# The front of a two-layer transformer kernel, put in another order on every engine

## The chip, the cores and the metric

One Trainium2 chip; the kernel uses one of its cores. The metric is the device time of one execution in microseconds (us), lower is better. All data are float32.

## What is computed

Layer 0 takes x of shape 4 x 1024 x 128 (four chunks of 1024 rows), normalises each row to xn and adds two branches to x: causal attention with 16 heads of 64, and a gated feed-forward block with integer weights.

```python
xn = _layernorm(x)                              # (x - mean) / sqrt(var + eps)
qkv = einsum('bse,ehd->bshd', xn, qkv_w) + qkv_b
attn = softmax(where(mask, q @ k / 8, -large)) @ v
x = x + attn @ out_w + out_b \
      + (silu(xn @ wg.T) * (xn @ wu.T)) @ wd.T  # wg, wu, wd = int / 127, 384 hidden columns
```

Layer 1 (a linear attention with a delta rule, and eight experts of which two are used) follows it. The change does not touch it.

## The kernel before

Every engine has its own list of instructions, written out by hand; semaphores join them. The change lies in the *front* of layer 0: what comes ahead of unit 0 of the attention. The attention has 32 units (4 chunks x 8 pairs of heads), each a call of `unit(u)` on every engine.

The front does the following for each chunk b = 0 to 3; a hidden block is (b, j) with j = 0, 1, 2 (three blocks of 128 of the 384 hidden columns).

- SyncE issues all loads in a fixed order: x of chunk 0 in halves, the integer weights, small rows, x of chunks 1 to 3, `outb_bc`, `w_qk` (two loads, `qk_loaded`), `w_v` and `bv_bc` (`v_loaded`), and so on.
- VectorE `statistics(b)`: mean and variance of the eight groups of 128 rows (L763, L767). GpSimd `deviation(b)`: variance plus eps, to the power -0.5 (L342, L344). VectorE `norm(b)`: eight tensor_scalar (L793) write xn. For chunk 0, `first_half`, `first_deviation` and `first_norm` do this in halves already.
- TensorE `flip_xn(b)`: eight transposes (L890), four into PSUM bank `flips[0]`, four into `flips[1]`. ScalarE `keep_hi(b)` copies each half to `hi_T` rounded to float32r (L534), VectorE `keep_lo(b)` writes the remainder `lo_T` (L805), ScalarE `keep_xnT(b)` the full value to `xnT` (L521, L522) for the attention. For chunk 0, `lo_T` comes from GpSimd (L354).
- TensorE `hidden(b, j)`: a gate product into `pair[0]`, then an up product into `pair[1]`. Each is two matmuls of 512 columns with `hi_T` (L914) and two with `lo_T` (L922); hidden(0,0) alone is in plain float32 (L910). ScalarE `silu(b, j)` reads `pair[0]` and writes `act_gate` (L540). VectorE `multiply(b, j)` multiplies `pair[1]` by it (L812). There is one `act_gate` and one pair of banks, so the next gate product waits for the silu, the next silu and the next up product wait for the multiply.
- TensorE `branch(b, halves)`: the down projection of a chunk, 12 small matmuls for each half (L936), into the two `flips` banks (chunk 3: `accum`). VectorE `add_branch` adds each half to x (L819, `ffn_added`). GpSimd `add_bias(b)` adds `out_b` to x first (L348). `flip_xn(b)` for b >= 2 waits for the additions of chunk b - 2, which free the two banks. The branches of chunks 2 and 3 run inside unit 0.
- TensorE `project(0, c, half)` (L959) and `project_values(0, i)` (L972): the six projections of unit 0, all through the one bank `misc`. Their readers are `keep_part` (ScalarE L444 or VectorE L606) and `keep_values` (VectorE L633); each projection waits for the reader of the one ahead of it. unit 0 starts with `project(1, 0, 1)` and then the scores (L994).

Of the kernel before, what the change touches and what calls it, by code (L numbers as in the profile page):

```python
# [6 lines left out]
F32 = mybir.dt.float32  # L7
# [3 lines left out]
ALU = mybir.AluOpType  # L11
ACT = mybir.ActivationFunctionType
# [4 lines left out]
B, S = 4, 1024  # L17
# [135 lines left out]
def layer0(block, sem, sbuf, kept, early, shared, b2_sb, x, qkv_w, qkv_b, out_w, out_b, w_gate, w_up, w_down, ln_w, ln_b, w_slow, w_out, Wg, b1, late):  # L153
# [55 lines left out]
    with ctx:  # L209
# [110 lines left out]
        def _(pool):  # L320
# [19 lines left out]
            def deviation(b):  # L340
                pool.wait_ge(var_ready, b + 1)
                pool.tensor_tensor(rstd[:, b, :], mv[:, b, :, 1], eps[:], ALU.add).then_inc(pool_step, 1)  # L342
                pool.wait_ge(pool_step, b + 2)
                pool.tensor_tensor(rstd[:, b, :], rstd[:, b, :], minus_half[:], ALU.pow).then_inc(rstd_ready, 1)  # L344

            def add_bias(b):
                pool.wait_ge(xn_ready, min(b + 2, B))
                pool.tensor_tensor(x1[:, b, :, :], x1[:, b, :, :],  # L348
                                   outb_bc[:].unsqueeze(1).broadcast_to([P, ROWS, E]), ALU.add).then_inc(xob_ready, 1)
# [3 lines left out]
            pool.wait_ge(hi_kept, 1)  # L353
            pool.tensor_tensor(lo_T[0][:], xnT[:, 0, :], hi_T[0][:].bitcast(F32), ALU.subtract).then_inc(lo_pool, 1)  # L354
            pool.wait_ge(small_loaded, 16)
            for b in range(1, B):
                deviation(b)
                add_bias(b - 1)
            add_bias(B - 1)

# [55 lines left out]
        def _(act):  # L416
# [100 lines left out]
            def keep_xnT(b):  # L517
                act.wait_ge(xn_flipped, 2 * b + 2)
                if b:
                    act.wait_ge(lo_dve, 2 * b)  # L520
                    act.activation(xnT[:, b, 0:512], flips[0][:], ACT.Copy)  # L521
                act.activation(xnT[:, b, 512:1024], flips[1][:], ACT.Copy).then_inc(xnT_act, 1)  # L522

            def keep_hi(b):
                if b == 0:
                    act.wait_ge(xnT_dve, 1)
                    act.wait_ge(xnT_act, 1)
                    act.activation(hi_T[0][:], xnT[:, 0, :], ACT.Copy).then_inc(hi_kept, 1)
                    return
                if b >= 2:  # L530
                    act.wait_ge(up_ready, NHID * (b - 1))
                for f in range(2):
                    act.wait_ge(xn_flipped, 2 * b + f + 1)
                    act.activation(hi_T[b % 2][:, 512 * f:512 * (f + 1)], flips[f][:], ACT.Copy).then_inc(hi_kept, 1)  # L534

            def silu(b, j):
# [3 lines left out]
                act.activation(act_gate[:], pair[0][:], ACT.Silu, scale=INT_SCALE).then_inc(silu_ready, 1)  # L540

            act.wait_ge(ints_loaded, 48)
            act.activation(raw_f[:, 0:2, :], raw[:, 0:2, :], ACT.Copy)
# [17 lines left out]
            keep_xnT(2)  # L561
            act.wait_ge(bq_scaled, 1)
            silu(2, 0)
            silu(2, 1)
            keep_hi(3)
            silu(2, 2)
            keep_xnT(3)
            silu(3, 0)
            keep_part(0, 1, 1)
            silu(3, 1)  # L570
            keep_part(0, 0, 0)
            silu(3, 2)
            for u in range(UNITS):
# [4 lines left out]
        def _(dve):  # L578
# [208 lines left out]

            def norm(b):
                dve.wait_ge(rstd_ready, b + 1)
                if b >= 2:  # L790
                    dve.wait_ge(xn_flipped, 2 * (b - 1))
                for r in range(ROWS):
                    last = dve.tensor_scalar(xn[:, b % 2, r, :], x1[:, b, r, :], mv[:, b, r, 0:1], rstd[:, b, r:r + 1],  # L793
                                             ALU.subtract, ALU.mult)
                last.then_inc(xn_ready, 1)
# [4 lines left out]

            def keep_lo(b):
                for f in range(2):
                    part = slice(512 * f, 512 * (f + 1))
                    dve.wait_ge(hi_kept, 2 * b + f)
                    dve.tensor_tensor(lo_T[b % 2][:, part], flips[f][:], hi_T[b % 2][:, part].bitcast(F32), ALU.subtract).then_inc(lo_dve, 1)  # L805

# [23 lines left out]
            dve.tensor_scalar(bq8, bq8, SCALE, None, ALU.mult).then_inc(bq_scaled, 1)  # L830
            statistics(1)
            multiply(0, 0)
            norm(1)
            multiply(0, 1)
            keep_lo(1)
            statistics(2)
            multiply(0, 2)
            norm(2)
            multiply(1, 0)
            add_branch(0, (0,))  # L840
            multiply(1, 1)
            add_branch(0, (1,))
            keep_lo(2)
            dve.wait_ge(v_loaded, 32)
            dve.wait_ge(bq_scaled, 1)
            statistics(3)
            multiply(1, 2)
            norm(3)
            multiply(2, 0)
            keep_part(0, 0, 1)  # L850
            add_branch(1, (0,))
            multiply(2, 1)
            add_branch(1, (1,))
            keep_part(0, 1, 0)
            keep_lo(3)
            multiply(2, 2)
            keep_values(0, 0)
# [9 lines left out]
        def _(pe):  # L867
# [12 lines left out]

            def flip_xn(b):
                if b:
                    pe.wait_ge(xn_ready, b + 1)
                if b >= 2:
                    pe.wait_ge(ffn_added, 2 * (b - 1))
                for f in range(2):
                    if b == 0:
                        pe.wait_ge((xn_first, xn_ready)[f], 1)
                    for r in range(GB):
                        last = pe.transpose(flips[f][:, P * r:P * (r + 1)], xn[:, b % 2, GB * f + r, :], ident[:])  # L890
                    last.then_inc(xn_flipped, 1)

            def hidden(b, j):
                n = b * NHID + j
                for h, w_T in enumerate((gate_T, up_T)):
                    if h == 0 and n:
# [235 lines left out]
            hidden(0, 0)  # L1132
            hidden(0, 1)
            flip_xn(1)
            hidden(0, 2)
            hidden(1, 0)
            pe.wait_ge(xnT_act, 2)
            branch(0, (0,))
            hidden(1, 1)
            branch(0, (1,))  # L1140
            flip_xn(2)
            hidden(1, 2)
            pe.wait_ge(qk_loaded, 32)
            pe.wait_ge(v_loaded, 32)
            project(0, 0, 1)
            hidden(2, 0)
            pe.wait_ge(xnT_act, 3)
            branch(1, (0,))
            hidden(2, 1)
            branch(1, (1,))  # L1150
            project(0, 1, 0)
            flip_xn(3)
            hidden(2, 2)
            project_values(0, 0)
            pe.wait_ge(xnT_act, 4)
            hidden(3, 0)
            project_values(0, 1)
            project(0, 1, 1)
            hidden(3, 1)
            project(0, 0, 0)  # L1160
            hidden(3, 2)
            pe.wait_ge(outw_loaded, 16)
# [2089 lines left out]
```

## Time and profile before

| what | value |
|---|---|
| time, median of 3 runs | 1658.24 us (1657.25 to 1658.27) |
| time of the profiled execution | 1658.69 us |
| its span | 1657.0 us |
| TensorE busy over the span | 1636.4 us (99%) |
| VectorE, ScalarE, GpSimd busy | 1328.9, 1006.7, 888.1 us |
| first transpose of xn | 9.44 us |
| first score of unit 0 | 66.78 us |

The profile is one execution on the chip. Busy time of TensorE counts each matmul to its modelled end, so two matmuls in a row overlap a little; a timeline row gives the start of a group, the time until the end of its last instruction, the engine, the line, what it writes and reads, the number of instructions (a float32 matmul is counted once for each of its passes), and in brackets how long the engine was idle before it and what ended that.

### The profile page before, as it was taken

How to read it: one execution, taken by the hardware profiler on the slowest of the kernel's cores; microseconds unless marked ns; L12 is line 12 of the kernel's file. 1: busy time of each engine (PE TensorE's matmuls, PEld its weight loads, DVE VectorE, ACT ScalarE, POOL GpSimd, SP SyncE). 2: the span in 40 equal slices, each digit the busy share in tenths (PEclk: the TensorE clock that was granted, in tenths of full speed). 3: DMA queues.
4: the chain of work that ended last, by engine and by line, in shares of the span. 5: the costliest groups of instructions: out<-in, count | busy, mean ns of one | idle time of the engine just before them, and what ended most of it. 6: DMA issues, size and time to landing. Idle time of an engine off the chain costs nothing.

```text
span 1657.0 us, 29205 instructions
## 1 busy us (share of the span) xinstructions
PE 1636.4 (99%) x9922; PEld 1043.9 (63%) x9922; DVE 1328.9 (80%) x2763; ACT 1006.7 (61%) x2025; POOL 888.1 (54%) x686
## 2 busy tenths in 40 slices
PE   8999999999999999999999999999999999999998
PEld 6756556655665566566656665665666767676767
DVE  6677777777777778777777777776999999999997
ACT  4456666656665666566656666666676657566562
POOL 3233333334333333433333433334999999999995
PEclk9999999999999999999999999999999999999999
DMA  8000000000000000000000000000000000000000
GB/s 182 26 1 1 2 1 1 1 2 1 1 1 1 1 2 1 1 1 1 1 1 1 1 2 1 1 27 1 1 1 7 7 1 8 5 4 7 1 8 13
DMA packets 30036, 13.55 MB, mean 8 GB/s; under 512 B 17066, under 2 KB 29380, under 8 KB 29892
## 3 DMA queue, kind: packets, MB, share of 16 engines
q1 hardware_dynamic: 29892, 11.70, 3.0%
q8 instruction: 82, 1.34, 0.3%
q14 instruction: 62, 0.51, 0.1%
HBM read 9.60 MB, written 2.10 MB: 7 GB/s over the span
## 4 chain that ended last, share of the span: by engine, by line
PE 92%; DVE 4%; ACT 1%; issue 1%; POOL 1%; DMA 0%; SPq 0%; DVEq 0%; ACTq 0%; POOLq 0%
PE pair L994 17%; PE flip L1011 16%; PE accum L1032 11%; PE pair L2739 8%; PE misc L959 7%; PE flip L2762 4%; PE misc L1078 4%; PE flip L2751 4%; PE misc L972 3%; PE accum L1056 3%; PE flip L2799 3%; PE accum L2751 2%; PE accum L2762 2%; PE accum L1060 2%; PE flip L2785 1%; PE flip L936 1%
## 5 line engine op out<-in xcount | busy, mean ns | idle before, releaser
L388 POOL TENSOR_SCALAR probs<-probs,recip 128x256 f32<-128x256 f32 (+5 forms) x448 | 331.3, 754 | 687.5 <-DVE recip L642 687.4
L463 ACT ACTIVATE probs<-pair,neg_max 128x768 f32<-128x768 f32 (+5 forms) x448 | 332.0, 749 | 208.4 <-DVE neg_max L624 208.4
L624 DVE TENSOR_REDUCE neg_max<-pair 128x1 f32<-128x768 f32 (+7 forms) x512 | 372.8, 754 | 31.4 <-PE pair L994 9.5
L1011 PEld LDWEIGHTS flip<-ident,probs 128*128 128x128 f32 x2048 | 228.0, 141 | 142.3 <-issue 64.7
L994 PE MATMUL pair<-qk_sb 64*128 64x512 f32 (+3 forms) x1536 | 291.6, 505 | 1.4 <-ACT probs L463 0.7
L1011 PE MATMUL flip<-ident,probs 128*128 128x128 f32 x2048 | 280.0, 277 | 1.8 <-ACT slots L425 1.8
L425 ACT ACTIVATE slots<-flip 128x512 f32<-128x512 f32 x320 | 183.6, 595 | 155.5 <-PE flip L1011 155.5
L615 DVE TENSOR_TENSOR pair<-pair,mask 128x128 f32<-128x128 f32 x512 | 137.2, 292 | 80.4 <-PE pair L994 80.3
L1032 PE MATMUL accum<-slots,v_sb 128*64 128x512 f32 (+3 forms) x1024 | 192.7, 519 | 0.0
L2739 PE MATMUL pair<-slow_sb,h_T 128*128 128x512 f32 x384 | 180.0, 594 | 1.2 <-ACT probs_last L463 1.0
L1571 POOL TENSOR_TENSOR prod<-xnT,qs 128x1024 f32<-128x1024 f32 (+3 forms) x32 | 180.2, 5638 | 0.9 <-DVE qs L2280 0.9
L994 PEld LDWEIGHTS pair<-qk_sb 64*128 64x128 f32 x1536 | 123.0, 186 | 69.3 <-issue 44.6
L1032 PEld LDWEIGHTS accum<-slots,v_sb 128*64 128x64 f32 x1024 | 67.9, 136 | 136.9 <-issue 132.3
L587 DVE COPY slots<-flip 128x512 f32<-128x512 f32 x192 | 131.9, 687 | 21.2 <-PE flip L1011 18.3
L959 PE MATMUL misc<-xnT,w_qk 128*128 128x512 f32 x256 | 134.3, 606 | 1.2 <-DVE v_sb L633 1.2
L2739 PEld LDWEIGHTS pair<-slow_sb,h_T 128*128 128x128 f32 x384 | 69.4, 190 | 74.1 <-issue 66.3
L1563 POOL TENSOR_TENSOR prod<-xnT 128x1024 f32<-128x1024 f32 (+2 forms) x24 | 109.2, 4551 | 10.5 <-DVE xnT L2280 10.2
L1609 POOL TENSOR_TENSOR terms<-terms 128x1024 f32<-128x1024 f32 x42 | 99.3, 2365 | 3.2 <-DVE terms L2366 1.2
L2762 PEld LDWEIGHTS flip<-w_qk,hid 128*128 128x128 f32 x736 | 87.3, 192 | 13.7 <-issue 8.4
L2762 PE MATMUL flip<-w_qk,hid 128*128 128x128 f32 x736 | 90.5, 276 | 0.2
L463 ACT ACTIVATION_READ_ACCUMULATOR probs<-pair,neg_max 128x1 f32 x448 | 90.5, 202 | 0.0
L2320 DVE TENSOR_REDUCE misc<-prod 128x16 f32<-128x1024 f32 (+3 forms) x32 | 90.2, 2818 | 0.0
(230 smaller groups left out, 2539.7 us busy)
## 6 DMA issues: line engine op xcount, KB each, us to landing
out<-x SPq DMA_DIRECT2D x8, 256.0 KB, 2.3
x<-in_L_attn_x SPq DMA_DIRECT2D x3, 512.0 KB, 5.8
slow_sb<-in_L_attn_w_slow SPq DMA_DIRECT2D x3, 512.0 KB, 7.5
w_qk<-in_L_attn_qkv_w SPq DMA_DIRECT2D x2, 512.0 KB, 7.2
xn<-in_L_ffn_W SPq DMA_DIRECT2D x1, 1024.0 KB
x<-in_L_attn_x SPq DMA_DIRECT2D x2, 256.0 KB, 3.3
w_v<-in_L_attn_qkv_w SPq DMA_DIRECT2D x1, 512.0 KB, 7.5
bv_bc<-in_L_attn_qkv_b SPq DMA_DIRECT2D x1, 512.0 KB, 7.5
```

The costliest lines, as they stand in the source:

```text
L388: pool.tensor_scalar(part, part, recip[:, u % 2, row, h:h + 1], 0.0, ALU.mult, ALU.add).then_inc(scaled, 1)
L425: act.activation(slot_rows(step, h, f), flips[bank][:].rearrange("p (k q) -> p k q", q=P), ACT.Copy).then_inc(flip_kept[bank], 1)
L463: act.activation(dst, pair[h][:, lo:hi], ACT.Exp, bias=neg_max[:, u % 2, row, h:h + 1], accum_out=row_sum[:, u % 2, row, h:h + 1]).then_in ...
L615: dve.tensor_tensor(pair[h][:, hi - P:hi], pair[h][:, hi - P:hi], mask[:], ALU.add).then_inc(covered, 1)
L624: dve.tensor_reduce(out=neg_max[:, u % 2, row, h:h + 1], in_=pair[h][:, lo:hi], axis=AX.X, op=ALU.max, negate=True).then_inc(max_ready, 1)
L959: pe.matmul(misc[:], lhsT=w_qk[:, c, P * n:P * (n + 1)], rhs=xnT[:, u // PAIRS, 512 * half:512 * (half + 1)], start=True, stop=True).then_ ...
L994: last = pe.matmul(pair[h][:, a:z], lhsT=q[part, P * r:P * (r + 1)], rhs=k[part, a - lo:z - lo], start=True, stop=True)
L1011: last = pe.transpose(flips[bank][:, P * k:P * (k + 1)], src[:, P * k:P * (k + 1)], ident[:])
L1032: last = pe.matmul(accum[D * h:D * (h + 1), at:512], lhsT=values_of(u, k, h), rhs=slots[:, base + at:base + 512], start=k == 0, stop=k == ...
L1571: pool.tensor_tensor(prod[s % 2][:, s:2 * s + 1, :], ks[:, 0:s + 1, :], qs[:, s % 2:s % 2 + 1, :].broadcast_to([P, s + 1, HD]), ALU.mult). ...
L2739: last = pe.matmul(places[k][:, 512 * half:512 * (half + 1)], lhsT=h_T[:, P * s:P * (s + 1)], rhs=slow_sb[:, c, 512 * half:512 * (half + 1 ...
L2762: last = pe.matmul(places[k][:, P * s:P * (s + 1)], lhsT=hid[:, e % 2, j, P * s:P * (s + 1)], rhs=w2_sb[:, e, j, :], start=j == 0, stop=j ...
```

## The change

The arithmetic is the same. The lists of the front are put in another order on every engine:

- VectorE: `norm` and `keep_lo` take one half at a time (the steps stand next to each other still; each half has its own semaphore count). `statistics(2)` moves from behind `keep_lo(1)` to a place ahead of `multiply(0,0)`, `statistics(3)` from behind `keep_lo(2)` to one behind `multiply(0,2)`. `keep_part(0,0,1)` and `keep_part(0,1,0)` move forward.
- TensorE: `flip_xn(b)` waits for each half of `norm` and for each half's bank alone. A `hidden` block can be issued as gate and up product apart: the transposes of chunk 1 stand between gate and up of (0,2); the second halves of the branches of chunks 0 and 1 stand between gate and up of (1,1) and (2,1), ahead of the up product; the transposes of chunks 2 and 3 come behind that up product. The projections of unit 0 are at other places, the last one, `project(0,0,0)`, at the very end.
- ScalarE: a Silu of one column of `ident` stands first. `keep_part(0,1,1)` and `keep_part(0,0,0)` come each one silu later.
- GpSimd: `deviation(1)` and `deviation(2)` come ahead of the biases; the biases wait for their own chunk's norm only.

```diff
--- before.py
+++ after.py
@@ -344,7 +344,7 @@
                 pool.tensor_tensor(rstd[:, b, :], rstd[:, b, :], minus_half[:], ALU.pow).then_inc(rstd_ready, 1)
 
             def add_bias(b):
-                pool.wait_ge(xn_ready, min(b + 2, B))
+                pool.wait_ge(xn_ready, 2 * b + 1)
                 pool.tensor_tensor(x1[:, b, :, :], x1[:, b, :, :],
                                    outb_bc[:].unsqueeze(1).broadcast_to([P, ROWS, E]), ALU.add).then_inc(xob_ready, 1)
 
@@ -352,11 +352,14 @@
             first_deviation(1)
             pool.wait_ge(hi_kept, 1)
             pool.tensor_tensor(lo_T[0][:], xnT[:, 0, :], hi_T[0][:].bitcast(F32), ALU.subtract).then_inc(lo_pool, 1)
+            deviation(1)
+            deviation(2)
             pool.wait_ge(small_loaded, 16)
-            for b in range(1, B):
-                deviation(b)
-                add_bias(b - 1)
-            add_bias(B - 1)
+            add_bias(0)
+            add_bias(1)
+            deviation(3)
+            add_bias(2)
+            add_bias(3)
 
             def constants():
                 pool.memset(earlier[:], 1.0).then_inc(earlier_step, 1)
@@ -521,7 +524,7 @@
                     act.activation(xnT[:, b, 0:512], flips[0][:], ACT.Copy)
                 act.activation(xnT[:, b, 512:1024], flips[1][:], ACT.Copy).then_inc(xnT_act, 1)
 
-            def keep_hi(b):
+            def keep_hi(b, halves=(0, 1)):
                 if b == 0:
                     act.wait_ge(xnT_dve, 1)
                     act.wait_ge(xnT_act, 1)
@@ -529,7 +532,7 @@
                     return
                 if b >= 2:
                     act.wait_ge(up_ready, NHID * (b - 1))
-                for f in range(2):
+                for f in halves:
                     act.wait_ge(xn_flipped, 2 * b + f + 1)
                     act.activation(hi_T[b % 2][:, 512 * f:512 * (f + 1)], flips[f][:], ACT.Copy).then_inc(hi_kept, 1)
 
@@ -539,6 +542,8 @@
                     act.wait_ge(hid_kept, b * NHID + j)
                 act.activation(act_gate[:], pair[0][:], ACT.Silu, scale=INT_SCALE).then_inc(silu_ready, 1)
 
+            act.wait_ge(ident_made, 1)
+            act.activation(act_gate[:, 0:1], ident[:, 0:1], ACT.Silu)
             act.wait_ge(ints_loaded, 48)
             act.activation(raw_f[:, 0:2, :], raw[:, 0:2, :], ACT.Copy)
             act.activation(raw_f[:, 2, :], raw[:, 2, :], ACT.Copy, scale=INT_SCALE * INT_SCALE).then_inc(ints_scaled, 1)
@@ -559,17 +564,17 @@
             keep_hi(2)
             silu(1, 2)
             keep_xnT(2)
-            act.wait_ge(bq_scaled, 1)
             silu(2, 0)
             silu(2, 1)
             keep_hi(3)
             silu(2, 2)
             keep_xnT(3)
+            act.wait_ge(bq_scaled, 1)
             silu(3, 0)
+            silu(3, 1)
             keep_part(0, 1, 1)
-            silu(3, 1)
+            silu(3, 2)
             keep_part(0, 0, 0)
-            silu(3, 2)
             for u in range(UNITS):
                 unit(u)
             tails["scalar"] = keep_flip, keep_att
@@ -785,11 +790,11 @@
                                              ALU.subtract, ALU.mult)
                 last.then_inc((xn_first, xn_ready)[f], 1)
 
-            def norm(b):
+            def norm(b, f):
                 dve.wait_ge(rstd_ready, b + 1)
                 if b >= 2:
                     dve.wait_ge(xn_flipped, 2 * (b - 1))
-                for r in range(ROWS):
+                for r in range(GB * f, GB * (f + 1)):
                     last = dve.tensor_scalar(xn[:, b % 2, r, :], x1[:, b, r, :], mv[:, b, r, 0:1], rstd[:, b, r:r + 1],
                                              ALU.subtract, ALU.mult)
                 last.then_inc(xn_ready, 1)
@@ -798,11 +803,10 @@
                 dve.wait_ge(xn_flipped, 2 * b + 1)
                 dve.tensor_copy(xnT[:, b, 0:512], flips[0][:]).then_inc(xnT_dve, 1)
 
-            def keep_lo(b):
-                for f in range(2):
-                    part = slice(512 * f, 512 * (f + 1))
-                    dve.wait_ge(hi_kept, 2 * b + f)
-                    dve.tensor_tensor(lo_T[b % 2][:, part], flips[f][:], hi_T[b % 2][:, part].bitcast(F32), ALU.subtract).then_inc(lo_dve, 1)
+            def keep_lo(b, f):
+                part = slice(512 * f, 512 * (f + 1))
+                dve.wait_ge(hi_kept, 2 * b + f)
+                dve.tensor_tensor(lo_T[b % 2][:, part], flips[f][:], hi_T[b % 2][:, part].bitcast(F32), ALU.subtract).then_inc(lo_dve, 1)
 
             def multiply(b, j):
                 dve.wait_ge(silu_ready, b * NHID + j + 1)
@@ -829,31 +833,37 @@
             dve.wait_ge(columns_kept, 1)
             dve.tensor_scalar(bq8, bq8, SCALE, None, ALU.mult).then_inc(bq_scaled, 1)
             statistics(1)
+            statistics(2)
             multiply(0, 0)
-            norm(1)
+            norm(1, 0)
+            norm(1, 1)
             multiply(0, 1)
-            keep_lo(1)
-            statistics(2)
+            keep_lo(1, 0)
+            keep_lo(1, 1)
             multiply(0, 2)
-            norm(2)
+            statistics(3)
+            norm(2, 0)
+            norm(2, 1)
             multiply(1, 0)
             add_branch(0, (0,))
+            dve.wait_ge(bq_scaled, 1)
+            keep_part(0, 0, 1)
+            add_branch(0, (1,))
             multiply(1, 1)
-            add_branch(0, (1,))
-            keep_lo(2)
+            keep_lo(2, 0)
+            keep_lo(2, 1)
+            multiply(1, 2)
+            norm(3, 0)
+            norm(3, 1)
+            multiply(2, 0)
+            add_branch(1, (0,))
+            keep_part(0, 1, 0)
+            add_branch(1, (1,))
+            multiply(2, 1)
+            keep_lo(3, 0)
+            keep_lo(3, 1)
+            multiply(2, 2)
             dve.wait_ge(v_loaded, 32)
-            dve.wait_ge(bq_scaled, 1)
-            statistics(3)
-            multiply(1, 2)
-            norm(3)
-            multiply(2, 0)
-            keep_part(0, 0, 1)
-            add_branch(1, (0,))
-            multiply(2, 1)
-            add_branch(1, (1,))
-            keep_part(0, 1, 0)
-            keep_lo(3)
-            multiply(2, 2)
             keep_values(0, 0)
             multiply(3, 0)
             keep_values(0, 1)
@@ -878,21 +888,24 @@
                 pe.transpose(pair[1][:, j * P:(j + 1) * P], raw_f[:, 2, j * P:(j + 1) * P], ident[:])
             pe.transpose(pair[1][:, 512:512 + COLUMNS], stage[:], ident[0:COLUMNS, 0:COLUMNS]).then_inc(setup_flipped, 1)
 
-            def flip_xn(b):
-                if b:
-                    pe.wait_ge(xn_ready, b + 1)
-                if b >= 2:
-                    pe.wait_ge(ffn_added, 2 * (b - 1))
-                for f in range(2):
+            def flip_xn(b, halves=(0, 1)):
+                for f in halves:
                     if b == 0:
                         pe.wait_ge((xn_first, xn_ready)[f], 1)
+                    else:
+                        pe.wait_ge(xn_ready, 2 * b + f)
+                    if b == 1:
+                        pe.wait_ge((xnT_dve, xnT_act)[f], 1)
+                    elif b:
+                        pe.wait_ge(ffn_added, 2 * (b - 2) + f + 1)
                     for r in range(GB):
                         last = pe.transpose(flips[f][:, P * r:P * (r + 1)], xn[:, b % 2, GB * f + r, :], ident[:])
                     last.then_inc(xn_flipped, 1)
 
-            def hidden(b, j):
+            def hidden(b, j, products=(0, 1)):
                 n = b * NHID + j
-                for h, w_T in enumerate((gate_T, up_T)):
+                for h in products:
+                    w_T = (gate_T, up_T)[h]
                     if h == 0 and n:
                         pe.wait_ge(silu_ready, n)
                     elif h and n:
@@ -1131,34 +1144,37 @@
             flip_xn(0)
             hidden(0, 0)
             hidden(0, 1)
+            hidden(0, 2, (0,))
             flip_xn(1)
-            hidden(0, 2)
+            hidden(0, 2, (1,))
+            pe.wait_ge(qk_loaded, 32)
+            project(0, 0, 1)
             hidden(1, 0)
             pe.wait_ge(xnT_act, 2)
             branch(0, (0,))
-            hidden(1, 1)
+            hidden(1, 1, (0,))
             branch(0, (1,))
+            hidden(1, 1, (1,))
             flip_xn(2)
             hidden(1, 2)
-            pe.wait_ge(qk_loaded, 32)
-            pe.wait_ge(v_loaded, 32)
-            project(0, 0, 1)
+            project(0, 1, 0)
             hidden(2, 0)
             pe.wait_ge(xnT_act, 3)
             branch(1, (0,))
-            hidden(2, 1)
+            hidden(2, 1, (0,))
             branch(1, (1,))
-            project(0, 1, 0)
+            hidden(2, 1, (1,))
             flip_xn(3)
             hidden(2, 2)
+            pe.wait_ge(v_loaded, 32)
             project_values(0, 0)
-            pe.wait_ge(xnT_act, 4)
             hidden(3, 0)
             project_values(0, 1)
+            hidden(3, 1)
             project(0, 1, 1)
-            hidden(3, 1)
+            hidden(3, 2)
             project(0, 0, 0)
-            hidden(3, 2)
+            pe.wait_ge(xnT_act, 4)
             pe.wait_ge(outw_loaded, 16)
             for u in range(UNITS):
                 unit(u)
```

## Rows read from the trace of the kernel before

**Rows 1.** Windows: us, busy by engine (x instructions), clock, DMA share, GB/s.

```profile
25.00:29.00 4.00, 3.97 (x17) 3.58 (x18) 3.08 (x9) 1.02 (x1) 1.74 (x2) 0.58 1.21 222
9.44:66.78 57.34, 48.62 (x243) 36.17 (x243) 37.41 (x102) 24.84 (x33) 18.73 (x15) 0.97 0.59 121
100.00:200.00 100.00, 100.00 (x643) 60.38 (x643) 74.39 (x163) 62.03 (x144) 35.07 (x48) 1.00 0.01 1
```

**Rows 2.** Timeline of TensorE in the front: start, us, then as told above.

```profile
14.88 0.73 PE L914 MATMUL pair<-hi_T,gate_T 128*128 128x512 f32 x2 [0.24 <-ACT act_gate L540]
...
19.03 1.09 PE L890 MATMUL flip<-ident,xn 128*128 128x128 f32 x8 [1.69 <-DVE xn L793]
19.88 0.71 PE L914 MATMUL pair<-hi_T,gate_T 128*128 128x512 f32 x2
...
25.03 1.22 PE L914 MATMUL pair<-hi_T,up_T 128*128 128x512 f32 x2 [1.67 <-DVE slots L812]
...
32.15 2.84 PE L936 MATMUL flip<-down_T,slots 128*128 128x128 f32 x24
35.93 1.06 PE L890 MATMUL flip<-ident,xn 128*128 128x128 f32 x8 [0.95 <-DVE x L819]
...
41.97 0.73 PE L914 MATMUL pair<-hi_T,up_T 128*128 128x512 f32 x2 [1.31 <-DVE slots L812]
...
47.55 2.84 PE L936 MATMUL flip<-down_T,slots 128*128 128x128 f32 x24
50.22 1.02 PE L959 MATMUL misc<-xnT,w_qk 128*128 128x512 f32 x2
...
62.41 1.02 PE L959 MATMUL misc<-xnT,w_qk 128*128 128x512 f32 x2
...
65.14 1.02 PE L959 MATMUL misc<-xnT,w_qk 128*128 128x512 f32 x2
66.78 1.99 PE L994 MATMUL pair<-qk_sb 64*128 64x512 f32 x8 [0.63 <-issue]
```

**Rows 3.** Timeline of ScalarE in the front.

```profile
12.51 1.28 ACT L540 ACT_TABLE_LOAD   x1
13.80 1.02 ACT L540 ACTIVATE act_gate<-pair 128x1024 f32<-128x1024 f32 x1
...
21.09 1.03 ACT L540 ACTIVATE act_gate<-pair 128x1024 f32<-128x1024 f32 x1 [0.28 <-PE pair L922]
...
63.48 0.69 ACT L444 ACTIVATE qk_sb<-misc,columns 128x512 f32<-128x512 f32 x1 [0.77 <-PE misc L959]
```

**Rows 4.** Timeline of VectorE in the front.

```profile
14.86 1.23 DVE L812 TENSOR_TENSOR slots<-pair,act_gate 128x1024 f32<-128x1024 f32 x1 [1.49 <-ACT act_gate L540]
16.83 2.14 DVE L793 TENSOR_SCALAR xn<-x,mv,rstd 128x128 f32<-128x128 f32 x8 [0.74 <-POOL rstd L344]
...
20.35 1.29 DVE L805 TENSOR_TENSOR lo_T<-flip,hi_T 128x512 fp32r<-128x512 f32 x2 [0.25 <-ACT hi_T L534]
21.56 1.64 DVE L763 BATCH_NORM_STATS2 stats<-x 128x6 f32<-128x128 f32 x8
...
23.79 1.19 DVE L812 TENSOR_TENSOR slots<-pair,act_gate 128x1024 f32<-128x1024 f32 x1
```

**Rows 5.** Timeline of GpSimd in the front.

```profile
15.16 1.64 POOL L344 TENSOR_TENSOR rstd<-rstd,minus_half 128x8 f32<-128x8 f32 x1
```

**Rows 6.** Loads of chunks 1 to 3, and of w_qk (second half).

```profile
L302 SPq DMA_DIRECT2D x<-in_L_attn_x x3: 393/574/1587, 6.2 to 7.2; - x3
...
DMA to landing us min/median/max: 4.4/5.8/6.9
...
11.21 2.95 SPq L305 DMA_DIRECT2D w_qk<-in_L_attn_qkv_w  x1
...
w_qk<-in_L_attn_qkv_w SPq DMA_DIRECT2D x1, 512.0 KB, 8.1
```

**Rows 7.** Line 784 from 6.6 to 7.84 us (ns min/median/max).

```profile
L784 DVE TENSOR_SCALAR xn<-x,mv,rstd x4: 343/348/350, 6.6 to 7.4; 128x128 f32<-128x128 f32 x4
```

## The prediction

> **What bounds the kernel now.** I read busy time and granted clock by stretches first, then TensorE's timeline, then the other engines' over the same stretch. From 100 to 200 us TensorE is busy for all of the 100 us [rows 1]: there the kernel ends when TensorE has worked through its list, so what is saved ahead of that list is saved at the end. The front, from the first transpose of xn at 9.44 us to the first score of unit 0 at 66.78, is different: TensorE is busy for 48.62 of 57.34 us, and from 25 to 29 us its mean clock was 0.58 of full speed, which costs 4.0 x 0.42 = 1.7 us [rows 1]. Its timeline shows the stops in brackets: 1.69 us for the xn of chunk 1, 1.67 us for a multiply of VectorE, 0.95 for a branch addition, 1.31 for another multiply [rows 2]. All changed lines are in this front, and behind it every engine has the list that it had. So the question is when the first score of unit 0 starts, against 66.78.
>
> **Prices of TensorE's work**, from start to start in full flow. A projection and a whole hidden block are 65.14 - 62.41 = 2.73 us, half a branch 50.22 - 47.55 = 2.67, the transposes of a chunk 19.88 - 19.03 = 0.85 [rows 2]. A projection ends 1.02 after its start, 0.16 of that as the tail that the next one overlaps (a two-pass row starts again 0.43 later twice): 0.86. So a hidden block is 1.87, one of its two products (gate or up, high and low part) 0.94; a value projection moves as many columns as a projection, 0.86. After a stop, the flow runs about 0.1 behind these: up(2,0), two half branches and a block are 8.15 by them and took 50.22 - 41.97 = 8.25.
>
> **Prices of the hand-overs.** Gate start to silu start 21.09 - 19.88 = 1.21, and the same from up start to a multiply that waits for it; silu to multiply 14.86 - 13.80 = 1.06; silu to the next gate 14.88 - 13.80 = 1.08; multiply to the up product behind it 25.03 - 23.79 = 1.24 [rows 2 to 4]. VectorE: statistics 23.79 - 21.56 = 2.23, norm 2.14 less 0.09 overlap = 2.05, a half 1.03; both lo_T halves 21.56 - 20.35 = 1.21; a multiply 1.23, less the same overlap 1.14 [rows 4].
>
> **ScalarE's table.** The one-column Silu loads Silu's table while ScalarE waits for the integers, and the load of 1.28 us at 12.51 goes [rows 3]. silu(0,0) then starts with the gate product instead of at 13.80. On the path it gives at most the 0.24 us that TensorE waited at 14.88 [rows 2], and the next stop takes that back.
>
> **Statistics moved.** statistics(1) ends at 14.86 - 1.49 = 13.37 [rows 4]. statistics(2) now follows it, until 15.53, ahead of multiply(0,0), which slips from 14.86. A loss of 0.67 for up(0,1): 15.53 + 1.24 = 16.77; silu(0,1) 16.85, gate(0,2) 17.93. The norm of chunk 1 does not slip: it had waited 0.74 us for rstd until 16.83 [rows 4], and VectorE is free at 16.67. So norm(1) stands at 16.83, multiply(0,1) at 18.88 as before; there the loss ends. This holds if x of chunk 2 has landed by 13.3: the loads of chunks 1 to 3 are issued between 6.2 and 7.2 and land 4.4, 5.8 and 6.9 us later, the middle one about 12.4 [rows 6]. Spare 0.9.
>
> **First turn of TensorE.** gate(0,2), now ahead of the transposes, runs 17.93 to 18.87, the transposes to 19.72 (their first half is ready at 17.9, the second at 18.9), up(0,2) waits for multiply(0,1): 18.88 + 1.24 = 20.12. The transposes come 0.16 earlier than before, so hi_T is done at 21.09 - 0.28 - 0.16 = 20.65, where silu(0,2) starts, and lo_T at 21.40 [rows 3, 4]. multiply(0,2) no longer stands behind statistics(2): 20.65 + 1.06 = 21.7 instead of 23.79. TensorE meanwhile does up(0,2) to 21.06, the projection moved here to 21.92 (the second half of w_qk is issued at 11.21 and takes 8.1, there by 19.3 [rows 6]) and gate(1,0) to 22.86. up(1,0) starts at 21.7 + 1.24 = 22.9 and was at 25.03: 2.1 us, with a projection of 0.86 already done. Lead 3.0.
>
> **From 23.84 on** I walked every wait of the new lists. TensorE's work up to the last projection of unit 0 is four half branches 10.68, four single products 3.76, six hidden blocks 11.22, five projections 4.30, two sets of transposes 1.70, together 31.66: to 55.5 if nothing waits. The narrow places:
> First, multiply(1,0) stands behind statistics(3) and norm(2): 22.84 + 2.23 + 2.05 = 27.1, so up(1,1) could start at 28.4. TensorE has both half branches and a gate in between and comes at 30.1. Spare 1.8.
> Second, the second half of the transposes of a chunk needs the addition behind the half branch: 35.93 - 32.15 = 3.78 after that branch starts [rows 2]. Between the two lie now the branch, an up product and half the transposes, 2.67 + 0.94 + 0.43 = 4.04. Spare 0.26, for chunks 2 and 3; before, TensorE stood for 3.78 - 2.67 = 1.1.
> Third, from a gate to the next up by way of silu and multiply it is 1.21 + 1.06 + 1.24 = 3.51. Between them lie gate, up, a projection or values, gate: 3 x 0.94 + 0.86 = 3.68. Spare 0.17, at up(2,0), (3,0), (3,1) and (3,2). At up(1,2) and (2,2) it is up to up, 1.21 + 1.24 = 2.45, against 0.94 + 0.85 + 0.94: spare 0.28. In the old list statistics(3) sat in such a gap, and TensorE stood for 1.31 at 41.97 [rows 2].
> Fourth, the tail. The last projection of unit 0 starts at 54.7; ScalarE begins to empty its bank 63.48 - 62.41 = 1.07 later and takes 0.69 [rows 2, 3]. The first projection of unit 1 needs that bank, with no hidden block in between as before: a new wait of 0.95, until 56.5. It is over at 57.4; multiply(3,2), which held the score back at 66.78, is done by 56.4.
>
> **Sum.** The score starts at 57.4, with 0.1 for each of three restarts at 57.7: 66.78 - 57.7 = 9.1 us. A cross-check by losses: before, 8.7 idle, 0.16 more of tail at each of ten stops, 1.7 for the clock, 12.0; after, 0.6 at the start, 1.35 before up(0,1), 0.2, 0.4, 0.04 and 0.95, 3.5: a gain of 8.5. I take the walk. The profiled execution lasted 1658.69 us, 1.7 around its span of 1657.0; less 9.1 that is 1649.6. It ran 0.45 above the median of the runs: 1649.1.
> Bounds: with no stop at all TensorE's 44.2 us of work from 9.5 would give 53.7, so 13 us is the most. Downwards, six narrow places that each miss by 0.2 cost 1.2.
>
> **Rivals.**
> The clock. It fell right after two stops of 1.69 and 1.67 us in 8 us [rows 1, 2]. The new order has one of 1.35, then gaps under 0.5, then 0.95 alone; the old one had 1.31 alone, at full clock behind it. So I expect no fall; one that stays costs the same 1.7 and gives 1650.8. The Trainium skill (TensorE: Matmul & The Clock Gate, section "HAM oscillation") says that bursts of matmuls with waits between them can run throttled again and again; by that rule this front stays at risk, for the same price, and this trace agrees with it once.
> The path that VectorE and GpSimd share. The power of deviation(2), 1.64 us [rows 5], now runs beside norm(1), which is on the path. If it held VectorE for its length, all behind slips: 1650.7. Against it: four norms that ran from 6.6 us, beside the power of chunk 0's second half, took 343 to 350 ns each [rows 7], eight with GpSimd idle 2.14 together, no less. The Trainium skill (SBUF — State Buffer, section "SBUF: two separate sides") calls this path an exclusive lock between a two-port VectorE operation and GpSimd; that is this rival, and the trace does not bear it out for the power.
> Slower. statistics(2) puts a load ahead of multiply(0,0) in VectorE's queue, and each us by which chunk 2 lands after 13.3 moves the whole front by one. Landing in 8.1 us like w_qk it would cost 1.4; it decides only past 26.0 (9.1 + 3.3 more). Nothing in [rows 6] comes near.
> Nothing gained. The lead would have to go again, 6 us of it: 14 us at 0.58 of the clock. Or unit 0 gives it back; but its waits are on engines that all come earlier by the same amount.
>
> **How the numbers follow.** Forecast (score between 56.7 and 58.7) 0.60, its own range 1648.1 to 1650.1; the clock 0.12; narrow places late or a wait that I missed, 1 to 4 us, 0.13; shared path 0.03; nothing gained 0.06; slower 0.03; more gained, through shorter early stops, 0.03. A measurement of this kernel tells about 0.2%, 3.3 us, from no change: faster 0.91, same 0.06, slower 0.03. The range takes in the clock, the shared path and most of the narrow places: 1646.9 to 1652.2.
>
> **What would show it.** One table load less and silu(0,0) ahead of 13.8; up(0,1) later, at 16.8; transposes of chunk 1 at 18.9; up(1,0) at 22.9; transposes of chunk 2 near 31.1; the score of unit 0 at 57.7, behind a wait of 0.8 to 0.95 us for ScalarE's qk_sb; granted clock 1.00 throughout. I am wrong if TensorE shows new waits for multiplies between 30 and 55 us, if the clock falls, or if the stretch from that score to the end is longer than the 1590.2 us of before.

## The result, and the profile after

The changed kernel takes 1652.78 us (median of 6 runs, 1651.76 to 1653.82) against 1658.05 us (6 runs, 1657.25 to 1659.37): a ratio of 0.9969, 95% interval 0.9959 to 0.9979. It is faster, by 5.3 us (0.3%), where 9.1 were forecast; the time lies 0.6 us above the range.

TensorE's timeline of the changed kernel, from the first transpose of xn; the lines answer to [rows 2]:

```profile
9.54 1.09 PE L902 MATMUL flip<-ident,xn 128*128 128x128 f32 x8
...
17.05 0.73 PE L927 MATMUL pair<-hi_T,up_T 128*128 128x512 f32 x2 [1.20 <-DVE slots L816]
...
19.21 0.60 PE L902 MATMUL flip<-ident,xn 128*128 128x128 f32 x4
21.30 0.66 PE L902 MATMUL flip<-ident,xn 128*128 128x128 f32 x4 [1.49 <-DVE xn L798]
22.43 0.84 PE L927 MATMUL pair<-hi_T,up_T 128*128 128x512 f32 x2 [0.48 <-DVE slots L816]
...
23.92 1.91 PE L972 MATMUL misc<-xnT,w_qk 128*128 128x512 f32 x2
...
26.88 0.63 PE L927 MATMUL pair<-hi_T,up_T 128*128 128x512 f32 x2
...
35.04 1.03 PE L902 MATMUL flip<-ident,xn 128*128 128x128 f32 x8
...
47.73 1.04 PE L902 MATMUL flip<-ident,xn 128*128 128x128 f32 x8
...
60.55 1.10 PE L972 MATMUL misc<-xnT,w_qk 128*128 128x512 f32 x2 [0.87 <-ACT qk_sb L447]
61.58 1.99 PE L1007 MATMUL pair<-qk_sb 64*128 64x512 f32 x8
```

The score of unit 0 starts at 61.58, not 57.7. Since the loads land earlier or later in each execution, I compare the *front* from here on: first transpose of xn to first score, in the one profiled execution of each kernel. It was 57.34 us, the walk said 57.7 - 9.44 = 48.26, and it is 61.58 - 9.54 = 52.04. All of the 3.8 us too many arise before 26.88, where up(1,0) (the up product of block (1,0)) starts, forecast for 22.9. Behind it the walk holds: from there to the score it said 34.8 us and it took 34.7, with no stop but the one of 0.87 in the tail. The stops that [rows 2] show before the transposes of chunk 2 and before up(2,0) are gone.

What went wrong before 26.88 is in two other timelines. VectorE's:

```profile
13.56 1.65 DVE L768 BATCH_NORM_STATS2 stats<-x 128x6 f32<-128x128 f32 x8
...
15.80 1.19 DVE L816 TENSOR_TENSOR slots<-pair,act_gate 128x1024 f32<-128x1024 f32 x1
16.97 4.28 DVE L798 TENSOR_SCALAR xn<-x,mv,rstd 128x128 f32<-128x128 f32 x8
21.17 1.21 DVE L816 TENSOR_TENSOR slots<-pair,act_gate 128x1024 f32<-128x1024 f32 x1
```

norm(1) takes 4.28 us, and took 2.14 [rows 4]. The same line from 18.6 to 19 us (ns, minimum, median, maximum) shows that it is one instruction:

```profile
L798 DVE TENSOR_SCALAR xn<-x,mv,rstd x2: 340/1406/2473, 18.5 to 18.8; 128x128 f32<-128x128 f32 x2
```

One tensor_scalar of 128 by 128 lasted 2473 ns; the one ahead of it took 340. GpSimd's timeline has what ran beside it:

```profile
17.18 1.72 POOL L344 TENSOR_TENSOR rstd<-rstd,minus_half 128x8 f32<-128x8 f32 x1
18.79 2.38 POOL L348 TENSOR_TENSOR x<-x,outb_bc 128x1024 f32<-128x1024 f32 x1
21.32 2.39 POOL L348 TENSOR_TENSOR x<-x,outb_bc 128x1024 f32<-128x1024 f32 x1 [0.16 <-DVE xn L798]
```

The bias of chunk 0 starts at 18.79 and ends at 21.17; the held instruction ends at 21.25, so it began at 18.78, within 0.01 us of the bias. Without the hold it would have ended at 16.97 + 2.14 = 19.11, that is, 0.3 us into the bias. The power of deviation(2), from 17.18, lay beside seven tensor_scalars of 337 to 347 ns and held none.

The clock fell as well. TensorE alone, in windows of 1 us (length, busy time with the instructions, granted clock, DMA share, GB/s):

```profile
20.00:21.00 1.00, 0.00 (x0) 1.00 1.32 216
22.00:23.00 1.00, 0.57 (x2) 0.95 1.00 196
23.00:24.00 1.00, 1.00 (x4) 0.50 1.04 223
25.00:26.00 1.00, 1.00 (x2) 0.50 1.23 259
26.00:27.00 1.00, 1.00 (x5) 0.84 1.37 230
```

It is at 0.50, the 1.2 GHz level, from just before 23 to about 26.3 us, behind a stretch in which TensorE stood for 1.49 and 0.48 us. Of the six executions three have a mean clock of 0.999 and spans of 1651.0 to 1651.1 us, three 1.000 and 1649.5 to 1649.8: a fall comes in some, and costs about 1.5 us. The profiled one is of the first kind; where the other two have theirs, no trace shows.

### The profile page after: what moved, and what is told of

Read it like the earlier page. It is cut to its first block, busy times and chain, and to the rows that moved or that the text cites. A ratio compares the mean times of both kernels' runs of the same rounds, so it can differ in the third digit from the quotient of the medians.

```text
span 1651.1 us, 29212 instructions
## 1 busy us (share of the span) xinstructions
PE 1635.6 (99%) x9922; PEld 1044.6 (63%) x9922; DVE 1330.1 (81%) x2763; ACT 1005.6 (61%) x2025; POOL 888.1 (54%) x686
## 4 chain that ended last, share of the span: by engine, by line
PE 96%; DVE 2%; ACT 1%; issue 1%; POOL 0%; DVEq 0%; POOLq 0%; ACTq 0%
PE pair L1007 17%; PE flip L1024 17%; PE accum L1045 11%; PE pair L2755 9%; PE misc L972 7%; PE flip L2778 5%; PE misc L1091 4%; PE flip L2767 4%; PE misc L985 3%; PE accum L1069 3%; PE flip L2815 3%; PE accum L2767 2%; PE accum L2778 2%; PE accum L1073 2%; PE flip L2801 1%; PE flip L949 1%
```

## The experiments

Ten kernels ran. Theory A: a tensor_scalar of norm(1) that meets the bias of GpSimd waits until this ends (2.2 us on the path), and the stops behind that let the clock fall (1.6 us). Rival B: the power of deviation(2) does it. The table has the measured values: medians over all runs of a kernel, and the rest from its one profiled execution. The expectations and edits follow. The kernel before ran beside the experiments too, with medians of 1658.2 to 1658.7 us.

| kernel | median us (runs) | front us | norm(1) us | held instruction ns |
|---|---|---|---|---|
| before | 1658.05 (6) | 57.34 | 2.14 | none |
| changed | 1652.78 (6) | 52.04 | 4.28 | 2473 |
| e1_bias_held | 1650.07 (5) | 48.42 | 2.14 | none |
| e2_bias_first | 1652.77 (5) | 51.97 | 4.20 | 2401 |
| e3_old_bias_early | 1660.23 (11) | 58.62 | 4.16 | 2361 |
| e5_filled_stop | 1652.02 (5) | 50.48 | 4.31 | 2502 |
| e9_bias_in_halves | 1650.98 (5) | 49.36 | 3.20 | 1403 |
| e4_held_and_tail | 1649.49 (5) | 48.12 | 2.14 | none |
| e6_no_preload | 1649.97 (5) | 48.44 | 2.14 | none |
| e7_statistics_back | 1651.65 (5) | 50.14 | 2.14 | 1166, in norm(2) |
| e8_branch_whole | 1653.43 (5) | 50.65 | 2.15 | none |
| e10_third_statistics_back | 1651.57 (5) | 50.07 | 2.14 | none |

**e1_bias_held.**

```diff
             def add_bias(b):
-                pool.wait_ge(xn_ready, 2 * b + 1)
+                pool.wait_ge(xn_ready, 3 if b == 0 else 2 * b + 1)
```

> The changed kernel, with one wait moved: GpSimd's bias of chunk 0 waits until both halves of norm(1) are done. Theory A (the bias, 2.38 us long, shut VectorE out of one tensor_scalar of norm(1)): all eight take 0.34 us, norm(1) 2.1 us instead of 4.28, multiply(0,1) at 19.0 instead of 21.17, and the score of unit 0 at 59.4 if the half-clock stretch at 23 to 26 us stays, at 57.8 if it goes: median 1650.6 or about 1649.5. Rival B (the power of deviation(2), which still runs beside norm(1), does it): norm(1) stays at 4.2 us and the time at 1652.8.

VectorE and GpSimd in e1:

```profile
17.51 2.14 DVE L798 TENSOR_SCALAR xn<-x,mv,rstd 128x128 f32<-128x128 f32 x8
19.56 1.22 DVE L816 TENSOR_TENSOR slots<-pair,act_gate 128x1024 f32<-128x1024 f32 x1
```

```profile
17.72 1.72 POOL L344 TENSOR_TENSOR rstd<-rstd,minus_half 128x8 f32<-128x8 f32 x1
19.80 4.74 POOL L348 TENSOR_TENSOR x<-x,outb_bc 128x1024 f32<-128x1024 f32 x2 [0.36 <-DVE xn L798]
```

The power still runs beside norm(1), whose eight take 339 to 346 ns. B falls; the bias is the cause. The front is 48.42 us, 0.2 from the walk, and the mean clock was 1.000 in all five executions. The spans of the two profiled executions differ by 3.0 us only and not by the 3.6 of the fronts, since the first transpose came at 10.09 here and at 9.54 there. Ratio to the kernel before 0.9949 (0.9936 to 0.9961).

**e2_bias_first.** On GpSimd, the bias ahead of deviation(2):

```diff
             deviation(1)
-            deviation(2)
             pool.wait_ge(small_loaded, 16)
             add_bias(0)
+            deviation(2)
             add_bias(1)
```

> The changed kernel with the bias of chunk 0 ahead of deviation(2) on GpSimd, so that the bias and not the power runs beside the start of norm(1). Theory A: one tensor_scalar of norm(1), now an early one, takes 2.4 to 2.7 us, norm(1) again 4.3; time as the changed kernel, within 1 us of 1652.8. Rival B (it is the power): norm(1) 2.1 us, 2 to 4 us faster.

The held instruction is now the first of norm(1):

```profile
L798 DVE TENSOR_SCALAR xn<-x,mv,rstd x1: 2401/2401/2401, 16.8 to 16.8; 128x128 f32<-128x128 f32 x1
```

```profile
16.68 2.39 POOL L348 TENSOR_TENSOR x<-x,outb_bc 128x1024 f32<-128x1024 f32 x1
```

The bias ends at 19.07, and only then do the other seven follow, at 333 to 334 ns. As A said: the hold goes with the bias, wherever it meets the norm.

**e3_old_bias_early.** The kernel before, with that one wait taken from the change:

```diff
-                pool.wait_ge(xn_ready, min(b + 2, B))
+                pool.wait_ge(xn_ready, b + 1 if b == 0 else min(b + 2, B))
```

> The kernel before, with one wait changed: the bias of chunk 0 no longer waits for norm(1) but for norm(0), so it starts at 16.8 beside norm(1). Theory A: a tensor_scalar of norm(1) takes about 2.5 us, norm(1) 4.3 instead of 2.14, the transposes of chunk 1 at 21.2 instead of 19.03, and the kernel is 2 us slower (1660). Rival B: norm(1) 2.1, same time as before.

```profile
17.05 4.16 DVE L793 TENSOR_SCALAR xn<-x,mv,rstd 128x128 f32<-128x128 f32 x8 [0.76 <-POOL rstd L344]
```

```profile
21.26 1.97 PE L890 MATMUL flip<-ident,xn 128*128 128x128 f32 x8 [3.72 <-DVE xn L793]
```

1660.23 us against 1658.34 (16 runs), ratio 1.0010 (1.0001 to 1.0019): 1.9 slower. The profiled front is 1.3 us longer and not 2: the stop before the transposes grew from 1.69 to 3.72, but the one before up(1,0) shrank from 1.67 to 0.33, and the clock was at 0.50 from 20 to 26 us (in before from 25 to 28). By itself this line of the change is a loss, and it is enough for the hold. The old wait for the *next* norm had kept the two apart.

**e5_filled_stop.** The changed kernel; seven matmuls into the unused `accum` between the two halves of the transposes of chunk 1:

```diff
                     last.then_inc(xn_flipped, 1)
+                    if b == 1 and f == 0:
+                        for _ in range(7):
+                            pe.matmul(accum[:, 0:P], lhsT=ident[:], rhs=ident[:], start=True, stop=True)
```

> The changed kernel as it is, bias beside norm(1), with seven matmuls of ident by ident (about 1.5 us, result unused) between the two halves of the transposes of chunk 1, where TensorE stood 1.49 us. Theory A (the held tensor_scalar costs the path 2.2 us by itself, and the stops behind it let the clock fall, 1.6 us more): norm(1) stays 4.2 us, multiply(0,1) at 21.2, but the clock stays at 1.00 from 22 to 27 us, the score comes 1.6 us earlier than 61.58 and every timed execution has the short span, about 1649.5, so a median near 1651.9. Rival: the clock falls all the same, time as the changed kernel (1652.8) or later.

```profile
19.44 1.73 PE L906 MATMUL accum<-ident 128*128 128x128 f32 x14
21.12 0.66 PE L902 MATMUL flip<-ident,xn 128*128 128x128 f32 x4
22.25 0.73 PE L930 MATMUL pair<-hi_T,up_T 128*128 128x512 f32 x2 [0.47 <-DVE slots L816]
22.82 0.63 PE L938 MATMUL pair<-lo_T,up_T 128*128 128x512 f32 x2
23.29 1.02 PE L975 MATMUL misc<-xnT,w_qk 128*128 128x512 f32 x2
```

```profile
23.00:24.00 1.00, 1.00 (x5) 1.00 0.74 167
```

The hold stays (2502 ns), the clock does not fall in this front: it is at 1.00, and the projection's two passes take 1.02 us where they took 1.91. The front is 50.48 us, so that the clock is 52.04 - 50.48 = 1.56 and the hold 50.48 - 48.42 = 2.06 of the 3.6 us between the changed kernel and e1. The spans say the same: 1649.4 to 1650.4 us in the four executions of e5 with the full clock, 1649.5 to 1649.8 in the three of the changed kernel. The median fell by 0.8 us, as expected, since half of the changed kernel's executions had no fall; the runs of the two kernels overlap. I expected the full clock in every execution; the fifth (0.999, span 1651.5) has a fall that no trace places. By itself this run does not show that the filled stop kept the clock up, since half of the executions of the changed kernel have no fall either; more on this below.

**e9_bias_in_halves.** The changed kernel, each bias in two instructions of 128 by 512:

```diff
-                pool.tensor_tensor(x1[:, b, :, :], x1[:, b, :, :],
-                                   outb_bc[:].unsqueeze(1).broadcast_to([P, ROWS, E]), ALU.add).then_inc(xob_ready, 1)
+                for f in range(2):
+                    rows = x1[:, b, GB * f:GB * (f + 1), :]
+                    last = pool.tensor_tensor(rows, rows, outb_bc[:].unsqueeze(1).broadcast_to([P, GB, E]), ALU.add)
+                last.then_inc(xob_ready, 1)
```

> The changed kernel with every bias of GpSimd in two instructions of 128 by 512 instead of one of 128 by 1024; the first still starts beside the last tensor_scalars of norm(1), at 18.8 us. Theory A (a tensor_scalar that starts beside the bias waits until that one instruction of GpSimd ends): the held tensor_scalar takes about 1.2 + 0.1 us instead of 2.47, norm(1) 3.1 instead of 4.28, the front is 1.1 us shorter than the changed kernel's 52.0, and more if the clock stays up. Rival (VectorE is slowed in proportion while GpSimd works, or held for the whole bias): norm(1) 4.2 us as before, since the two halves together last as long.

```profile
L800 DVE TENSOR_SCALAR xn<-x,mv,rstd x2: 341/872/1403, 18.4 to 18.7; 128x128 f32<-128x128 f32 x2
```

```profile
18.68 5.04 POOL L350 TENSOR_TENSOR x<-x,outb_bc 128x512 f32<-128x512 f32 x4
```

One such half starts 5.04 / 4 = 1.26 us behind the one ahead of it and lasts 1.27 to 1.31, and the hold is 1.40: it ends with the one instruction of GpSimd, not with the bias. VectorE is not slowed in proportion, it waits for one instruction. The front is 2.7 us shorter than that of the changed kernel: 1.1 by the shorter hold, and the clock stayed up. This profiled execution has its clock fall outside the front:

```profile
1135.00:1140.00 5.00, 5.00 (x9) 0.67 0.01 3
```

**e4_held_and_tail.** e1, and in the tail:

```diff
-            hidden(3, 2)
+            hidden(3, 2, (0,))
             project(0, 0, 0)
+            hidden(3, 2, (1,))
```

> e1_bias_held, and in the tail the up product of (3,2) behind the last projection instead of ahead of it. The wait of 0.87 us of the first projection of unit 1 for ScalarE's qk_sb goes, but the multiply of (3,2) comes 0.86 later and then holds the score. By the walk the score comes 0.4 to 0.6 us earlier than in e1. Rival: the later multiply eats all of it, no difference to e1.

```profile
56.44 1.10 PE L972 MATMUL misc<-xnT,w_qk 128*128 128x512 f32 x2
57.95 1.99 PE L1007 MATMUL pair<-qk_sb 64*128 64x512 f32 x8 [0.40 <-issue]
```

The stop of 0.87 is gone and TensorE stands for 0.40 before the score. The profile names no releaser for it; the multiply of (3,2) ends at 57.85, 0.1 us ahead of the score. The front is 0.3 shorter, where I expected 0.4 to 0.6, the median 0.6 lower, 1649.49 us, ratio 0.9945 (0.9933 to 0.9958). It has the lowest median; against e1 the difference is less than the runs can tell.

**The other parts, each undone in e1.** e6 leaves out the one-column Silu:

```diff
-            act.wait_ge(ident_made, 1)
-            act.activation(act_gate[:, 0:1], ident[:, 0:1], ACT.Silu)
```

> e1_bias_held without the one-column Silu at the start of ScalarE's list. By the walk the table load comes back at 12.5 us and silu(0,0) at 13.9, before the place where VectorE's statistics(2) let multiply(0,0) run (15.8): no difference to e1_bias_held, within 0.3 us. Rival: the load was on the path, 1 us slower.

The load is back at 13.20, and TensorE stands for 0.24 and 0.87 us where it stood for 1.21 at once; the front is 48.44 against 48.42. Nothing, as expected.

e7 puts statistics(2) back (and, on GpSimd, deviation(2) behind the first bias):

```diff
             statistics(1)
-            statistics(2)
             multiply(0, 0)
...
             keep_lo(1, 1)
+            statistics(2)
             multiply(0, 2)
```

> e1_bias_held with statistics(2) back behind the lo_T of chunk 1 and deviation(2) behind the first bias. By the walk up(0,1) comes 0.7 earlier but multiply(0,2) 2.2 later, about 24 us, so TensorE waits 2 us for it before up(1,0): score 2.1 later than e1 if the clock stays, 3.5 if it falls; median 1652.2 to 1653.7. Rival: the stop is absorbed by work moved there, below 1 us.

```profile
25.04 0.73 PE L927 MATMUL pair<-hi_T,up_T 128*128 128x512 f32 x2 [1.53 <-DVE slots L816]
```

1.7 us of front and 1.6 in the median, where I expected 2.1 or more: the transposes' first half now starts with the first half of norm(1), lo_T is done 0.3 us sooner against the start of the front, and the statistics with it; I had not counted that. By the way it shows the hold once more, off the path: its norm(2) starts at 27.13 beside the second bias, and one tensor_scalar of eight lasts 1166 ns, until that bias is over.

```profile
L798 DVE TENSOR_SCALAR xn<-x,mv,rstd x8: 333/336/1166, 27.1 to 29.8; 128x128 f32<-128x128 f32 x8
```

```profile
25.86 2.35 POOL L348 TENSOR_TENSOR x<-x,outb_bc 128x1024 f32<-128x1024 f32 x1
```

e8 keeps the blocks (1,1) and (2,1) whole:

```diff
-            hidden(1, 1, (0,))
+            hidden(1, 1)
             branch(0, (1,))
-            hidden(1, 1, (1,))
```

(the branch of chunk 1 likewise; on VectorE multiply(1,1) and (2,1) ahead of the second addition)

> e1_bias_held with the gate and up products of (1,1) and (2,1) together again ahead of the second half branch (and VectorE's multiply ahead of the addition). By the walk TensorE then waits 1.1 us before the second half of the transposes needs the addition, less 0.4 because the first half no longer waits, for two chunks: 1.4 to 2.2 us slower than e1. Rival: no difference.

```profile
29.00 0.73 PE L927 MATMUL pair<-hi_T,up_T 128*128 128x512 f32 x2 [0.58 <-DVE slots L816]
...
33.83 0.63 PE L902 MATMUL flip<-ident,xn 128*128 128x128 f32 x4 [0.51 <-DVE x L823]
```

2.2 us of front: half a microsecond and its tail for each pair of transposes, and a stop at up(1,1), since multiply(1,0) behind statistics(3) and norm(2) is no longer covered. I expected 1.4 to 2.2. The median is 3.4 higher; two of the five executions had a clock fall, the profiled one at 1135 to 1140 us as in e9, so the front is the better measure.

e10 puts statistics(3) back behind the lo_T of chunk 2 (and, on GpSimd, deviation(3) behind the bias of chunk 2; only VectorE's part is shown):

> e1_bias_held with statistics(3) back behind the lo_T of chunk 2, ahead of multiply(1,2), and deviation(3) behind the bias of chunk 2. By the walk multiply(1,2) comes 2.2 us later and TensorE, which had 0.14 to spare there, waits some 1.5 to 2.0 us before up(2,0): front 50.0 to 50.4 us instead of 48.4, median 1651.6 to 1652.1. Rival: the gap is covered by the projection that now lies there, under 1 us.

```diff
             multiply(0, 2)
-            statistics(3)
             norm(2, 0)
...
             keep_lo(2, 1)
+            statistics(3)
             multiply(1, 2)
```

```profile
38.10 0.73 PE L927 MATMUL pair<-hi_T,up_T 128*128 128x512 f32 x2 [1.37 <-DVE slots L816]
```

1.65 us of front, 1.5 in the median, as expected.

## Why the prediction was wrong

**The step that failed** is the sentence "So norm(1) stands at 16.83 and multiply(0,1) at 18.88 as before; there the loss ends". The start of norm(1) was right (16.97); its length was not: 4.28 us, where the sum has 2.05, and multiply(0,1) came at 21.17 instead of 18.88. The prediction has no term for the new wait of the bias, and I never wrote down when the bias now starts. The trace of before would have told: deviation(1) ends at 15.16 + 1.64 = 16.80 [rows 5], and deviation(2) took 24.23 + 1.65 - 23.95 = 1.93 there:

```profile
23.95 0.20 POOL L342 TENSOR_TENSOR rstd<-mv,eps 128x8 f32<-128x8 f32 x1 [2.50 <-DVE mv L767]
24.23 1.65 POOL L344 TENSOR_TENSOR rstd<-rstd,minus_half 128x8 f32<-128x8 f32 x1
```

The bias would follow at 18.7, while norm(1) runs until 18.9 by the forecast. They overlap by 0.2 us by these numbers and by 0.3 in the run, and that is enough, because the last tensor_scalar is not slowed for that time but held until the 2.38 us of the bias are over. The rival of the shared path was named, but with the wrong partner: I asked only about the power, which the trace rightly cleared, and gave the rival 0.03. [rows 4] could not warn, since in the old list the bias always waited for the next norm. The rule that I quoted did: the Trainium skill (SBUF — State Buffer, section "SBUF: two separate sides") says that whichever operation starts first keeps the path for its whole instruction, and that the other is blocked. For the bias the runs agree: in the changed kernel, e2, e3, e5 and e9 the held instruction ended about 0.1 us behind the instruction of GpSimd. For the power of 128 by 8 they do not: it ran 1.72 us beside tensor_scalars of normal length.

**The clock** was the second miss, a rival held at 0.12. Its size is 1.56 us by e5, 1.7 by my price. That it follows from the hold is supported, not proven, by where the fall lies in the profiles. It is between 20 and 29 us in before, the changed kernel, e2 and e3; it is not in the front of e1 and the five kernels built on it, which hold the bias back, nor in e5 (the hold with its stop filled) and e9 (half the hold). Over all executions, the mean clock is 0.999 in 7 of 11 of the changed kernel and e2, and in 3 of 30 of e1 and the five built on it. A mean of 0.999 alone does not tell the place: the falls of e8 and e9 lie at 1135 to 1140 us, and why they come there is open.

**The sum** was otherwise right. Without those two the front is 48.42 (e1) against 48.26. Point by point, forecast to measured: up(0,1) 16.77 to 17.05, transposes of chunk 1 18.9 to 19.2, up(1,0) to score 34.8 to 34.7, tail 0.95 to 0.87 idle, preload nothing (e6), clock at full to a fall. The places with 0.17 to 0.28 us to spare all held: TensorE has no stop there. One slip of arithmetic changes nothing: "slower" would have been decided past 13.3 + 9.1 + 3.3 = 25.7 us, not 26.0. The order of the branches is worth 2.2 us (e8), each moved statistics about 1.7 (e7, e10). Behind the score the changed kernel is 1651.1 - 61.58 = 1589.5 us, before 1590.2: some tenths more arose in layer 1, which I had set at none. They come with the change and not by chance: the stretch is 1589.5 to 1589.7 in the eight profiles of the changed kernel and its variants that have no fall there, 1590.1 in e3. No run was made for their cause.

**From the front to the time** the forecast was less good than the front alone says: e1, with a front 0.2 from the walk, has a median of 1650.07, 1.0 above the 1649.1 of the sum. Two things lie in this. I counted the 1.7 us of the clock as lost in every execution of before, and corrected for it only by the 0.45 between the profiled execution and the median; in the runs beside the experiments 18 of 34 executions of before have a mean clock of 0.999, the others 1.000. And the first transpose, which waits for the integer weights, came at 9.74 to 10.14 us in the six profiles that hold the bias back, at 9.32 to 9.64 in the other six. Nothing in the edits explains that, and no run settles whether it is chance.

## What to carry over

When a wait is changed, write down when the waiting instruction now *starts* and what the other engine that shares its path runs at that moment, even when its own result is wanted much later. A long GpSimd tensor_tensor can hold a short VectorE tensor_scalar until it ends, 2.1 us for an overlap of 0.3; an old wait that looks too strict may be what keeps them apart. And a stop made by such a hold can cost twice, when TensorE's clock falls behind it.

## What the runs showed of the hardware

- A tensor_scalar from SBUF to SBUF (128 by 128, float32) that meets a tensor_tensor of GpSimd (128 by 1024 or 128 by 512, SBUF to SBUF) waits for its end: 2473, 2401, 2361 and 2502 ns beside one of 2.35 to 2.40 us, 1403 beside one of 1.27 to 1.31, and 1166 where it came 1.27 us behind the start of one of 2.35. VectorE's multiply, which reads PSUM, ran beside the next bias in 1.21 us, as ever. No run shows the other order, a GpSimd instruction that waits.
- A GpSimd power of 128 by 8, 1.72 us long, held nothing beside norm(1); it took 1.64 where no tensor_scalar ran beside it. Why it differs from the bias, no run shows.
- A mean clock of 0.999 came in three of six executions of one kernel, with spans 1.2 to 1.6 us longer. In the profiles the stretch at 0.50 lies in the front in four kernels, and at 1135 to 1140 us in two.
- What a profiled execution tells: e1 and e6 differ only in what is off the path, and their fronts are 48.42 and 48.44 us; the five runs of e1 spread over 1.0 us.
